# Two attention layers and a mixture of experts on Trainium2: small blocks, idle products, and the way back as products of 512 and 256 columns

## The reference

```python
logits = x @ gate_w + gate_b
probs = softmax(logits)
top_w, top_idx = top_k(probs, 2)
top_w = top_w / sum(top_w)
h = silu(einsum('td,edf->tef', x, w1)) * einsum('td,edf->tef', x, w3)
out_e = einsum('tef,efd->ted', h, w2)
out = einsum('ted,te->td', out_e, combine)   # combine holds top_w at top_idx, else 0
```

## Time and profile before

| | |
|---|---|
| median of three timed runs | 2104.35 us (2102.48 to 2105.95) |
| the profiled execution's own time | 2097.15 us |
| its span, first to last instruction | 2095.4 us |
| TensorE busy | 1889.9 us (90%) |
| VectorE busy | 1563.5 us (75%) |
| ScalarE busy | 1157.6 us (55%) |
| GpSimd busy | 922.3 us (44%) |
| mean granted TensorE clock | 0.958 |

### The profile page before, as it was taken

How to read it: one execution, slowest core, us unless ns; L and a number is a source line. 1 busy time by engine, 2 the same in 40 slices (tenths; PEclk the granted TensorE clock), 3 DMA queues, 4 the chain that set the end, 5 groups by cost and what they waited for, 6 DMA issues and landing times. The chain is left out here.

```text
span 2095.4 us, 36022 instructions
## 1 busy us (share of the span) xinstructions
PE 1889.9 (90%) x11968; PEld 1327.3 (63%) x11968; DVE 1563.5 (75%) x3233; ACT 1157.6 (55%) x2414; POOL 922.3 (44%) x683
## 2 busy tenths in 40 slices
PE   4899999986589999999999999829999999999998
PEld 2566667764223434343434343329999999999998
DVE  7999999992466777777666777447777777777775
ACT  2356666654336555555555655426666666666663
POOL 6999999971533335343434431122222222222222
PEclk9999999997779999999999999859999999999999
DMA  5222222300515142424334250047676666666661
GB/s 173 112 92 112 112 100 101 139 4 23 122 34 121 46 106 72 111 89 92 99 79 106 64 127 32 21 159 225 225 230 218 217 224 225 222 225 225 222 215 60
DMA packets 140067, 271.47 MB, mean 130 GB/s; under 512 B 13915, under 2 KB 91823, under 8 KB 134066
## 3 DMA queue, kind: packets, MB, share of 16 engines
q1 hardware_dynamic: 128812, 244.55, 38.1%
q0 software_dynamic: 10624, 25.26, 3.2%
q10 hardware_dynamic: 518, 0.27, 0.0%
HBM read 201.96 MB, written 71.39 MB: 130 GB/s over the span
## 5 line engine op out<-in xcount | busy, mean ns | idle before, releaser
L1449 DVE CUSTOM_DVE_ANT_0 x_dump<-x_ps,x_bias_q 128x512 bf16<-128x512 f32 x512 | 353.1, 690 | 100.5 <-PE x_ps L1142 87.7
L1318 ACT ACTIVATE x_PT<-x_ps 128x512 f32<-128x512 f32 x512 | 292.5, 602 | 225.9 <-PE x_ps L1157 222.9
L1931 ACT ACTIVATE X<-m_ps 128x256 f32<-128x256 f32 x312 | 119.5, 383 | 226.5 <-PE m_ps L1868 226.4
L1835 POOL DMA_INDIRECT out_dram<-e_y,e_label x78 | 78.9, 1012 | 359.0 <-DVE e_y L1987 347.1
L1142 PE MATMUL x_ps<-x_KS,x_QS 96*128 96x512 bf16 x512 | 199.3, 391 | 25.8 <-DVE x_mx L1449 25.3
L1156 PE MATMUL x_ps<-x_bias_k,x_ident_b 128*128 128x512 bf16 x512 | 195.5, 382 | 2.8 <-DMA x_QS<-x_rows 1.5
L1157 PE MATMUL x_ps<-x_QS,x_KS 98*128 98x512 bf16 x512 | 195.2, 381 | 0.0
L1970 DVE TENSOR_TENSOR X<-X,m_ps 128x256 f32<-128x256 f32 x312 | 120.8, 417 | 97.9 <-ACT X L1931 93.3
L1868 PE MATMUL m_ps<-e_x_lo,m_hi 128*128 128x256 f32 x640 | 181.5, 284 | 1.5 <-DVE e_x_lo L1955 1.5
L1868 PE MATMUL m_ps<-e_x_hi,m_hi 128*128 128x256 f32 x640 | 181.3, 283 | 0.0
L1868 PE MATMUL m_ps<-e_x_hi,m_lo 128*128 128x256 f32 x640 | 181.2, 283 | 0.0
(11 more groups left out here) (309 smaller groups left out, 5451.9 us busy)
## 6 DMA issues: line engine op xcount, KB each, us to landing
m_raw<-in_L_ffn_w_dram SPq DMA_DIRECT2D x117, 1024.0 KB, 5.2
expert_in<-a_blank SPq DMA_DIRECT2D x34, 1032.0 KB, 4.3
parts<-x_part SPq DMA_DIRECT2D x24, 512.0 KB, 3.8
m_x<-expert_in SPq DMA_DIRECT2D x39, 258.0 KB, 4.8
next_mask_k<-in_maskT_dram SPq DMA_DIRECT2D x32, 256.0 KB, 2.7
next_mask_q<-in_mask_dram SPq DMA_DIRECT2D x29, 256.0 KB, 2.8
x_KS<-parts SPq DMA_DIRECT2D x16, 384.0 KB, 11.1
x_QS<-parts SPq DMA_DIRECT2D x8, 576.0 KB, 6.9
```

The source lines that it names most:

```text
L1318: act.activation(PT[unit % 2][:, k, :], ps_st[e % 3], ACT.Exp, scale=DH ** -0.5).then_inc(exp_done, 1)
L1449: dve.tensor_tensor_reduce(out=dump[:, :], in0=ps_max[m % 2], in1=bias_q[b % 2][:, q, :], scale=1.0, scalar=NEG, op0=ALU.add, op1=ALU.max, ...
L1931: act.activation(silu[f % 2], ps_h[f % 4][:, 0:BLK], ACT.Silu).then_inc(silu_done, 1)
```

## The change

It has four parts.

1. **Small blocks.** A block table has now 32 entries (`FULL`) of 256 rows and 7 (`HALF`) of 128 rows. Experts' rows are padded to a multiple of 128. The 39 slots are run in rounds of ten, of which the slots 4 and 9 are small (`ROUND`, `HALVES`): 10 written out, a loop of two rounds of ten, and 9 more written out. A small block has one tile of 128 rows instead of two: half the moving columns in `hidden`, half the products in `project`, half the transposes, half the width of the operations on ScalarE and VectorE, one gather and one scatter instead of two. Its weights are loaded and split as for a large one. The table is computed by 36 short operations instead of 22.
2. **The way back.** The high and low parts of w2 lie side by side (`w2_both`, [P, FC, 2, D]). The high part of the gated numbers is multiplied with both in one product of 512 columns, the low part with the high part in one of 256 columns. The result has two halves, and `add_y` adds each with an operation of its own, the second waiting for the first (`y_half`).
3. **Idle products.** TensorE issues plain f32 products of 128 columns of the identity with itself, whose results nobody reads: 6, 38, 9, 8, 6 and 6 before the transposes at units -14, -10, -8, -6, -4 and -2 (`BUSY_BEFORE`), four before `project_kv` at units -12 and -8, one after each of the 24 `scores_for_maximum` below unit 0; in the last sequence 2 before each of four outputs, 10 and 2 before the transposes for the gate, 3 before each of two sets of logits, 10 before the ranks (`BUSY_AT_LAST`); and 16 between attention and experts, after the high part of the first block's second weight tile.
4. TensorE waits for VectorE's first memset (`consts_v`) before the second attention, since the idle products write the bank that it clears.

```diff
-NBLK = T * TOPK // BLK + NE - 1
+FULL = T * TOPK // BLK
+HALF = NE - 1
+NBLK = FULL + HALF
+ROUND = 10
+HALVES = (4, 9)
...
+BUSY_BEFORE = {-14: 6, -10: 38, -8: 9, -6: 8, -4: 6, -2: 6}
...
+        final = TPB * (BATCH - 1)
+        BUSY_AT_LAST = {**{("output", final + j): 2 for j in range(TPB)}, ("turn", final // 2): 10, ("logits", final // 2): 3,
+                        ("turn", final // 2 + 1): 2, ("logits", final // 2 + 1): 3, ("ranks", BATCH - 1): 10}
...
+            def stay_busy(products, out):
+                for _ in range(products):
+                    pe.matmul(out, ident_f[:, :], ident_f[:, :], start=True, stop=True)
...
             def bank_m(event):
                 what, n = event
+                if event in BUSY_AT_LAST:
+                    stay_busy(BUSY_AT_LAST[event], ps_max[0][:, 0:P])
...
             pe.wait_ge(consts, 1)
+            pe.wait_ge(consts_v, 1)
...
                     if k == (1 if unit >= 0 else 3):
+                        if unit < 0:
+                            stay_busy(BUSY_BEFORE.get(unit, 0), ps_o[:, 0:P])
...
                     for m in islice(maxima, 1):
                         scores_for_maximum(m)
+                        if unit < 0:
+                            stay_busy(1, ps_o[:, 0:P])
...
+                if unit in (-12, -8):
+                    stay_busy(4, ps_o[:, 0:P])
                 for n in tiles_at(unit):
                     project_kv(n)
...
+def tiles_in(q):
+    return 1 if q % ROUND in HALVES else BT
...
+        w2_both = [sb("both0", [P, FC, 2, D], F32R), None]
...
+            @block.tensor
+            def _(pe):
+                pe.wait_ge(hi_done[1], 1)
+                for _ in range(16):
+                    pe.matmul(ps[:, 7, 0:P], ident_f[:, :], ident_f[:, :], start=True, stop=True)
...
+                dve.wait_ge(iotas, 4)
+                do(dve.tensor_copy(where[:, :, :], where_i[:, :, :]))
...
-                do(dve.tensor_tensor(past[:, :, :], starts[:, :, :], ends[:, :].unsqueeze(1).broadcast_to([1, NBLK, NE]), ALU.is_ge))
-                do(dve.tensor_reduce(n_past[:, :], past[:, :, :], AX.X, ALU.add))
...
+                do(dve.tensor_tensor(past[:, :, :, :], limit[:, :, :].unsqueeze(3).broadcast_to([1, 2, NBLK, NE]), wide(now), ALU.is_ge))
+                do(dve.tensor_reduce(n_past[:, :, :], past[:, :, :, :], AX.X, ALU.add))
+                do(dve.tensor_tensor(taken[:, :, :, :], past[:, :, :, :], wide(weight), ALU.mult))
+                do(dve.tensor_reduce(left[:, :, :], taken[:, :, :, :], AX.X, ALU.add))
...
+                def two_passes(out, left, both, first, last):
+                    order = ((1, D), (0, 2 * D)) if last else ((0, 2 * D), (1, D))
+                    for n, (a, columns) in enumerate(order):
+                        mm = pe.matmul(out[:, 0:columns], left[a], both[:, 0:columns], start=first and n == 0, stop=last and n == 1)
+                    return mm
...
-                                mm = three_passes(ps_h[f % 4][:, at:at + BLK],
+                                mm = three_passes(ps_h[f % 4][:, at:at + wide],
                                                   [w[p][n][:, c, f * P:(f + 1) * P] for w in (w_hi, w_lo)],
-                                                  [x_hi[p][:, c, :], x_lo[p][:, c, :]], c == 0, c == KC - 1)
+                                                  [x_hi[p][:, c, 0:wide], x_lo[p][:, c, 0:wide]], c == 0, c == KC - 1)
...
-                                mm = three_passes(ps_y[n], [g[:, f, n * P:(n + 1) * P] for g in (g_hi, g_lo)],
-                                                  [w[p][2][:, f, :] for w in (w_hi, w_lo)], f == 0, f == FC - 1)
+                                mm = two_passes(ps_y[n], [g[:, f, n * P:(n + 1) * P] for g in (g_hi, g_lo)],
+                                                w2_both[p][:, f, :, :].rearrange("p k d -> p (k d)"), f == 0, f == FC - 1)
...
-                        dve.scalar_tensor_tensor(out=yb[p][:, n, :], in0=ps_y[n], scalar=label[p][:, n, 0:1], in1=yb[p][:, n, :],
-                                                 op0=ALU.mult, op1=ALU.add).then_inc(y_left, 1)
+                        dve.scalar_tensor_tensor(out=yb[p][:, n, :], in0=ps_y[n][:, 0:D], scalar=label[p][:, n, 0:1], in1=yb[p][:, n, :],
+                                                 op0=ALU.mult, op1=ALU.add).then_inc(y_half, BT // tiles)
+                        dve.wait_ge(y_half, BT * j + (n + 1) * (BT // tiles))
+                        dve.scalar_tensor_tensor(out=yb[p][:, n, :], in0=ps_y[n][:, D:2 * D], scalar=label[p][:, n, 0:1], in1=yb[p][:, n, :],
+                                                 op0=ALU.mult, op1=ALU.add).then_inc(y_left, BT // tiles)
```

More of the change, by code:

```diff
@@ L1706, in experts @@
             sem_ = lambda n: route.enter_context(nc.semaphore("r_" + n))
-            starts_i, starts = sb("starts_i", [1, NBLK, NE], I32), sb("starts", [1, NBLK, NE])
-            per_e = lambda n, d=F32: sb(n, [1, NE], d)
-            total, total_i, padded_i, padded, ends = per_e("total"), per_e("total_i", I32), per_e("padded_i", I32), per_e("padded"), per_e("ends")
-            off = [per_e("off0"), per_e("off1")]
-            past, skipped = sb("past", [1, NBLK, NE]), sb("skipped", [1, NBLK, NE])
-            per_b = lambda n: sb(n, [1, NBLK])
-            n_past, sum_past, at, number = per_b("n_past"), per_b("sum_past"), per_b("at"), per_b("number")
+            both = lambda n, d=F32: sb(n, [1, 2, NE], d)
+            total, total_i = sb("total", [1, NE]), sb("total_i", [1, NE], I32)
+            rows_i, size, weight = both("rows_i", I32), both("size"), both("weight")
+            upto = [both("upto0"), both("upto1")]
+            past, taken = sb("past", [1, 2, NBLK, NE]), sb("taken", [1, 2, NBLK, NE])
+            where_i, where, limit = sb("where_i", [1, 2, NBLK], I32), sb("where", [1, 2, NBLK]), sb("limit", [1, 2, NBLK])
+            over, more, less = sb("over", [1, 1]), sb("more", [1, 1]), sb("less", [1, 1])
+            n_past, left, number = sb("n_past", [1, 2, NBLK]), sb("left", [1, 2, NBLK]), sb("number", [1, 2, NBLK])
+            odd, apart, chosen = sb("odd", [1, NBLK]), sb("apart", [1, 2, NBLK]), sb("chosen", [1, 2, NBLK])
             iotas, chain, blocks_known = sem_("iotas"), sem_("chain"), sem_("blocks_known")
@@ L1767, in _ @@
[L1767 to L1770 removed]
+                do(dve.tensor_scalar_add(total_i[:, :], total[:, :], float(P - 1)))
@@ new lines, in _ @@
+                do(dve.tensor_scalar(over[:, :], now[:, 0, NE - 1:NE], float(FULL * BLK), None, ALU.subtract))
+                do(dve.tensor_scalar(more[:, :], over[:, :], 0.0, None, ALU.max))
+                do(dve.tensor_scalar(less[:, :], over[:, :], -0.5, None, ALU.mult))
+                do(dve.tensor_copy(limit[:, 0, :], where[:, 0, :]))
+                do(dve.tensor_scalar(limit[:, 1, :], where[:, 1, :], less[:, 0:1], None, ALU.add))
+                do(dve.tensor_scalar(less[:, :], less[:, :], 0.0, None, ALU.max))
@@ new lines, in _ @@
+                do(dve.tensor_scalar(limit[:, 1, FULL:], where[:, 1, FULL:], less[:, 0:1], more[:, 0:1], ALU.add, ALU.subtract))
+                do(dve.tensor_scalar(weight[:, 0, :], size[:, 0, :], -1.0, None, ALU.mult))
+                do(dve.tensor_tensor(weight[:, 1, 0:NE - 1], size[:, 0, 1:NE], size[:, 0, 0:NE - 1], ALU.subtract))
+                do(dve.tensor_scalar(weight[:, 1, NE - 1:NE], size[:, 0, NE - 1:NE], -1.0, None, ALU.mult))
+                wide = lambda a: a[:, :, :].unsqueeze(2).broadcast_to([1, 2, NBLK, NE])
@@ L1789, in experts @@
             ps_h = [ps[:, 2 + n, :] for n in range(4)]
-            ps_y = [ps[:, 6 + n, 0:D] for n in range(2)]
+            ps_y = [ps[:, 6 + n, :] for n in range(2)]
             x_used = pair("x_used")
@@ L1911, in _ @@
-                hidden(LAST, LAST // 2, 0)
-                project(LAST, LAST // 2, 0)
+                                mm.then_inc(y_ps, BT // tiles)
+                turn(0, 0)
+                for q in range(ROUND):
+                    hidden(0, q)
+                    turn(0, q + 1)
+                    project(0, q)
+                with pe.Fori(1, ROUNDS) as i:
+                    for q in range(ROUND):
+                        hidden(i, q)
+                        turn(i, q + 1)
+                        project(i, q)
@@ L1948, in _ @@
-                hidden(LAST, 0, False)
+                    gated_high(j, FC // 2 - 1, wide)
+                x_high(0, 0)
+                for q in range(ROUND):
+                    hidden(0, q)
+                    x_high(0, q + 1)
+                with act.Fori(1, ROUNDS) as i:
+                    for q in range(ROUND):
+                        hidden(i, q)
+                        x_high(i, q + 1)
+                for q in REST:
+                    hidden(ROUNDS, q, q + 1 in REST)
+                    if q + 1 in REST:
+                        x_high(ROUNDS, q + 1)
@@ L1964, in gate @@
+                def gate(i, q, following=True):
```

(15 more changed lines are left out.)

260 lines of the change are left out of this document (126 added, 134 removed).

## The result

The changed kernel takes 2078.90 us (median of four runs, 2068.76 to 2096.53), the kernel before 2104.56 us in the same session: a ratio of 0.9888 [0.986, 0.9916]. The profiled execution took 2079.34 us, its span is 2077.5, against 2097.15 and 2095.4 before. So the time is inside the range on record (2044 to 2086) and on the forecast side, but the gain is 24 to 26 us by the medians and 18 in the two profiled executions, where the sum gave 40.

A forecast was written before the change was run, and what follows sets the result against it. The prediction took TensorE to bound the experts and chains across engines at its lower clock to bound the second attention's ends. Its terms summed to -39.7 us, 2064.6 from the median 2104.35; it predicted 2064, range 2044 to 2086.

The forecast's parts named there:

- the forecast case: Whole kernel: narrow products cost 0.118 us and idle products hold the clock; 2064 us, range 2050 to 2080, chance 0.62.
- Small blocks, -22 (-15 to -31): Experts: seven 128-row blocks take 14.2 us on TensorE instead of 17.36, -22 us in all.
- the four-column row: Trace row of four-column f32 products, 0.114 us each, taken to show that the stationary tile sets a narrow product's cost.
- rival on the narrow product: Experts' 128-column products: slow at 0.215 us, 2130 us in all, chance 0.10; or cheap below 0.1, 2055 us, chance 0.12.
- Way back, -8 (0 to -13): Experts' products back: a 512- and a 256-column product cost 0.338 us instead of 0.354 for three, -8 us over 32 large blocks.
- Last block's addition, +0.5: End of the experts: VectorE's second addition is covered in the other blocks; only the last block pays, +0.5 us.
- Table of blocks, +4.6: Between attention and experts: 36 VectorE operations instead of 22, plus a wait for four iotas, +4.6 us (3.5 to 6).
- Idle products at the start, -8 + 0.5: Start of the second attention: a held clock gives -8 us (0 to -14), the wait for VectorE's first memset +0.5.
- End, -5: End of the attention: outputs, transposes and gate logits go at a higher clock, -5 us (+1 to -6).
- Before the experts, -2.3: 16 products ahead of the experts: 3.1 us less at full clock, 0.8 us of delay, net -2.3 us.
- the clock is not held: Rival: in the second attention idle products run at 0.43 us and their gains are lost; -17, 2088 us, chance 0.12.
- far longer straight-line code: Rival in the experts: 29 blocks written out instead of 5, instruction fetches beside weight traffic; within 0.2%, chance 0.04.

The follow-up runs named there:

- after: The changed kernel itself, with all four parts of the change, against the kernel before: 2078.90 us, ratio 0.9888.
- short_loops: The changed kernel with small blocks last and large blocks in loops of two instead of ten: 2060.8 us, ratio to the kernel before 0.9807.
- all_loops: The changed kernel with small blocks last, large and small blocks both in loops of two, five blocks written out: 2068.35 us, ratio to the kernel before 0.9841.
- three_after: The changed kernel with three products of 256 columns and one addition on the way back: 2074.04 us, ratio to the kernel before 0.9860.
- idle_no_ramp: The kernel before plus the idle products, without those at the start of the second attention: 2098.32 us, ratio to the kernel before 0.9981.
- idle_no_tail: The kernel before plus the idle products, without those at the end of the second attention: 2095.04 us, ratio to the kernel before 0.9969.
- idle_no_16: The kernel before plus the idle products, without the 16 ahead of the experts: 2091.38 us, ratio to the kernel before 0.9944.
- idle_only: The kernel before with the idle products alone, its experts and table unchanged: 2088.58 us, ratio to the kernel before 0.9928.
- before: The kernel without the change, which every ratio is taken against: 2104.56 us in the session of the changed kernel.
- ten_last: The changed kernel with small blocks last, large blocks still in loops of ten: 2072.29 us, ratio to the kernel before 0.9851.
- short_three: short_loops with three products of 256 columns and one addition on the way back: 2066.05 us, ratio to the kernel before 0.9830.
- all_three: all_loops with three products of 256 columns and one addition on the way back: 2066.41 us, ratio to the kernel before 0.9817.

## Why the prediction was right, and where its steps were not

The time came within the range, faster than before as forecast; the forecast case (idle products fill waits, small blocks bound by the stationary side) is the one that happened. In the profiled executions the sum of -39.7 became -17.8: the mechanisms but the way back's are right, and that the total fell inside the range owes something to the range's width, since the two largest misses, the way back and the stalls, point the same way. One of the four runs (2096.53 us) lies outside it. By its steps:

- **Small blocks, -22 (-15 to -31): right.** 0.111 us per narrow product, where I took the 0.118 of 256 columns and the four-column row had 0.114; 13.94 us against 14.2, seven of them -24.0. Neither rival on the narrow product holds: not 0.215, and not below 0.1. Both loads and narrow products of this type came 111 ns apart. The Trainium skill's 81 ns (TensorE: Matmul & The Clock Gate, Back-to-back issue gap) do not hold for them; the measurement decides.
- **Way back, -8 (0 to -13): the step that failed by its size.** I took 0.220 us for 512 columns from bf16 products; rounded f32 took 0.23 followed by 0.12, the lower end of my bounds, "nothing". The bf16 row was of another type: the row that bore on it was the 256-column product of the same type, twice. What the form did give, up to 3 us, came through the pitch of the hidden products, and in after hardly at all.
- **Last block's addition, +0.5:** inside the noise; the end took 9.30 us after the last product instead of 9.22. VectorE's further additions cost no block anything in short_loops and all_loops, as argued; three_after, without them, keeps the stall at the jump. With a late gather they may cost something (block 37), which is not shown.
- **Table of blocks, +4.6: right,** +4.6 with the iotas' wait (four operations of 0.80 us, predicted 0.85).
- **Idle products at the start, -8 + 0.5: right,** -6.7 and, by idle_no_ramp, -6.8; the wait for the memset is +0.6. The 2.07 us that I took for a query projection from the earlier trace rows is an output projection's of the same shape. **End, -5:** -3.5, and -4.0 by idle_no_tail. **Before the experts, -2.3:** -1.7 (first block -2.7, start +1.0), and -2.0 by idle_no_16; the +1.0 isn't theirs, since idle_only goes from the table to the first hidden product in 20.7 us, before in 21.0. The rival "the clock is not held" is refuted by the windows.
- **Missing from the sum: +9.8 us of stalls in the experts,** which I had named as a rival ("far longer straight-line code", 0.04) and given no price. It is the largest piece of what is left. The stall at the jump (5.9 of the 9.8 us) is shown: the traces of the three kernels with loops of ten (after, three_after, ten_last) have it, 5.9, 5.8 and 3.2 us, and none of those with loops of two has. It is not the addition (three_after) and not the order of the blocks (ten_last). That TensorE's instructions came late there is read from "issue" and from the packets of the instruction queues. The late gather (3.9 us) follows a wait of GpSimd in written-out code, which all_loops takes away (32.7 to 5.4 us); why 5.6 us of it made a block late and 5.45 elsewhere didn't was not tried. Why after's four runs spread over 28 us stays open: all_loops has no stall in its profile, and its runs spread over 15. The 2096.53 us run left no trace.

The rest of the gap between 2057.5 us (the sum on the profiled execution) and 2079.34: 9.8 stalls, some 6.5 way back, 3.5 in the first layer, 3.5 smaller gains from idle products with the wait for the memset, 0.5 in the scores, less 2 for small blocks that were better than forecast: 21.8.

The best kernel of these by its median is short_loops, 2060.8 us, 0.9807: the change's parts with the loop kept at two blocks and the small blocks at the end. Its interval overlaps those of the other three with small blocks and loops of two (short_three, all_loops, all_three).

## What to carry to other kernels

Price the code, not only the work: where a change writes blocks out or makes a loop's body five times as long, look at each engine's "issue" waits and at the packets of the instruction queues, and put irregular blocks at one end, so that the regular ones keep a short loop. A few microseconds of waiting on TensorE can cost more through the clock than they last: 3.3 us of waiting made 9.9 in ten_last, 2.4 made 3.9 and 4.1 made 5.9 in after, 2.2 no more than 3.2 in ten_last. So a late gather on an engine off the path can take 10 us. Take the price of a new shape from rows of the same type, twice the narrower one before a wide one of another type. And filling waits with idle products pays where the waits had let the clock fall: about 0.7% here, from some 160 products.

## What the runs showed of the hardware that was not expected

- At a jump back over ten blocks' code TensorE stood for 4.14 us and VectorE for 5.55 (2.22 and 5.55 in ten_last), with nothing in the profile that held them; in no profile here did they at a jump over two. That their instructions came late is the reading, not a row.
- GpSimd stood for up to 5.8 us before a gather in written-out code with nothing that held it (ten_last); in loops of two mostly for 0.3, in before once for 2.3.
- The same hidden products run 113.4, 117.8, 118.6 or 120.0 ns apart, constant within a block. Which of them a block gets goes with the form of the way back before it and with small blocks before it; why, no run here shows. Behind a 512-column rounded f32 product the next starts after 224 to 240 ns, mostly 235.
- The runs of short_loops and of all_loops fall in two groups some 10 us apart, by their mean clock. The trace of a slower one (short_loops) and that of a quicker one (all_loops) agree in the experts to 0.5 us and differ in the attention's scores by 6.9 us (748.2 and 741.3), where the clock fell more often. Why some executions have this stays open.
